# A symmetric product of later batches: one quarter transposed in place of computed, and a bank for each half

## The reference

```python
x = x + attn(layernorm(x))          # linear attention: no softmax
    # theta, phi = x @ W_theta.T, x @ W_phi.T ; g = x @ W_g.T
    # attn = (theta @ phi.T / 16) @ g
x = x + ffn(layernorm(x))
    # rmsnorm, q/k/v (16 heads, 4 key heads of 16), rope,
    # causal softmax attention over the 1024 rows, wo,
    # rmsnorm, gate over 8 experts, top 2, SiLU expert blocks (512 wide)
```

## Time and profile before

| what | value |
|---|---|
| median of three runs | 1089.72 us (1089.57 to 1092.33) |
| the profiled execution | 1089.67 us, of which the span from first to last instruction is 1087.9 |
| PE busy | 1042.4 us (96%) |
| DVE busy | 763.2 us (70%) |
| ACT busy | 581.1 us (53%) |
| POOL busy | 421.9 us (39%) |
| HBM traffic | 55.76 MB read, 41.14 MB written |

### The profile page before, as it was taken

How to read it: one execution, slowest core, us unless ns; L and a number is a source line. 1 busy time by engine, 2 the same in 40 slices (tenths; PEclk the granted TensorE clock), 3 DMA queues, 4 the chain that set the end, 5 groups by cost and what they waited for, 6 DMA issues and landing times.

```text
span 1087.9 us, 19824 instructions
## 1 busy us (share of the span) xinstructions
PE 1042.4 (96%) x6630; PEld 619.5 (57%) x6630; DVE 763.2 (70%) x1811; ACT 581.1 (53%) x1124; POOL 421.9 (39%) x493
## 2 busy tenths in 40 slices
PE   7999999999999999999999999999999999999996
PEld 6765335564435333354333533456667986679996
DVE  4699999768788897788886699243485555555552
ACT  3563566646677887747666566641432244453320
POOL 2020232625643134521434512555637833344332
PEclk9999999999999999999999999999999999999999
DMA  6334113322324656723342511233434432222322
GB/s 192 124 94 122 51 49 106 93 76 77 100 75 140 187 175 193 216 78 99 105 126 85 140 55 37 65 75 74 103 83 98 99 62 38 45 36 40 50 43 27
DMA packets 85732, 101.50 MB, mean 93 GB/s; under 512 B 17632, under 2 KB 73312, under 8 KB 85632
## 3 DMA queue, kind: packets, MB, share of 16 engines
q1 hardware_dynamic: 70752, 80.60, 25.7%
q0 software_dynamic: 14880, 19.64, 9.5%
HBM read 55.76 MB, written 41.14 MB: 89 GB/s over the span
## 4 chain that ended last, share of the span: by engine, by line
PE 70%; DVE 19%; issue 4%; ACT 4%; POOL 1%; DMA 1%; SPq 0%; POOLq 0%; DVEq 0%; ACTq 0%
PE psum L2167 12%; PE psum L2189 9%; PE psum L2119 9%; PE psum L2152 8%; PE psum L2105 7%; DVE psum L1881 7%; PE psum L2085 4%; DVE mx L1883 3%; PE psum L2161 3%; PE psum L2071 3%; PE psum L2126 2%; PE psum L2088 2%; ACT probs_mem L1360 2%; PE psum L2092 2%; PE psum L2038 2%
## 5 line engine op out<-in xcount | busy, mean ns | idle before, releaser
L1360 ACT ACTIVATE probs_mem<-psum 128x512 f32<-128x512 f32 (+1 forms) x464 | 233.6, 585 | 103.3 <-PE psum L2105 98.6
L1881 DVE CUSTOM_DVE_ANT_1 psum<-psum,masking 128x640 f32<-128x640 f32 (+3 forms) x256 | 256.9, 1046 | 31.1 <-PE psum L2088 28.2
L2105 PE MATMUL psum<-stack_mem 98*128 98x512 bf16 (+3 forms) x768 | 170.9, 327 | 6.0 <-ACT probs_mem L1360 2.4
L1259 POOL DMA_INDIRECT out<-yout,labels x68 | 108.9, 1602 | 164.7 <-DVE yout L1961 78.1
L1200 POOL TENSOR_SCALAR_AFFINE_SELECT probs_mem<-probs_mem 128x512 f32<-128x512 f32 x104 | 67.7, 653 | 237.4 <-ACT probs_mem L1360 237.1
L2105 PEld LDWEIGHTS psum<-stack_mem 98*128 98x128 bf16 x768 | 65.0, 97 | 104.5 <-ACT probs_mem L1360 21.5
L1385 ACT ACTIVATE gated<-psum 128x512 f32<-128x512 f32 x68 | 40.6, 597 | 150.9 <-PE psum L2152 68.9
L2119 PE MATMUL psum<-probs_mem,v 128*17 128x512 f32 (+3 forms) x1152 | 116.0, 490 | 0.6 <-ACT heads_out L1367 0.2
L2189 PE MATMUL psum<-w_mem,gated 128*128 x480 | 114.4, 381 | 0.0
L1883 DVE TENSOR_REDUCE mx<-psum 128x4 f32<-128x512 f32 (+2 forms) x96 | 96.6, 1040 | 19.5 <-PE psum L2093 11.8
L2085 PE MATMUL psum<-stack_mem 96*128 96x512 bf16 x256 | 94.8, 383 | 8.6 <-DVE mx L1881 5.1
(11 more groups left out here) (243 smaller groups left out, 1770.1 us busy)
## 6 DMA issues: line engine op xcount, KB each, us to landing
block<-routed SPq DMA_DIRECT2D x68, 129.0 KB
w_mem<-in_w13T SPq DMA_DIRECT2D x16, 512.0 KB, 4.4
qk_parts<-w_mem SPq DMA_DIRECT2D x16, 384.0 KB, 2.6
stack_mem<-qk_parts SPq DMA_DIRECT2D x32, 192.0 KB, 3.0
w_mem<-in_x SPq DMA_DIRECT2D x8, 512.0 KB, 5.3
out<-w_mem SPq DMA_DIRECT2D x8, 512.0 KB, 4.1
x_late<-out SPq DMA_DIRECT2D x8, 512.0 KB, 5.0
stack_mem<-qk_parts SPq DMA_DIRECT2D x32, 128.0 KB, 2.6
```

The source lines that it names most:

```text
L1259: e.indirect_dma_start(out_rows, bass.IndirectOffsetOnAxis(ap=to, axis=0), youts[w % NYOUT], None, bounds_check=NBATCH * SEQ - 1, oob_is_e ...
L1360: e.activation(probs[probs_of(m)][:, hh:hh + n, q0:CH], grid(turn[step][0][:, 0:n * (CH - q0)], n), ACT.Exp, scale=float(HD) ** -0.5).then ...
L1881: e.tensor_tensor_reduce(keys, keys, masked(w), 1.0, -3e38, ALU.add, ALU.max, to).then_inc(sem["max"], 1)
L2105: m = e.matmul(bk[:, i * (CH - q0):(i + 1) * (CH - q0)], s[0:STACK + NMAX, kt // TPR, GRP, kt % TPR * P:(kt % TPR + 1) * P], s[0:STACK + N ...
```

## The change

For batches 1 to 3:

- The first step forms rows 0 to 127 of the Gram matrix as before, 8 products of 128x256.
- The second step forms only the right half of rows 128 to 255: 8 products of 128x128. The left half of these rows is the transpose of the right half of the first rows. Once ACT has copied the first half to SBUF, PE transposes that 128x128 quarter from there into the place in PSUM (one transposition; a new wait on `gram_out`).
- Each half lies in a bank of its own, so a later batch takes two neighbouring banks of the ring, both from before the first product to the copy of the second half.
- ACT copies each half for itself, 128x256, so it has two instructions where it had one, and `gram_out` counts both.
- The plan's costs of the two steps are new: 3.46 and 1.85 on PE in place of 3.46 each, and 0.29 on ACT for each in place of 0.49 once. `needs` is unchanged: the plan doesn't know that the second step waits for ACT's copy of the first half.

Batch 0 is as before; its two parts lay in two banks already.

```diff
--- before.py
+++ after.py
@@ -142,6 +142,8 @@
 
 def gram_steps(b):
 
+
+
     return KD if b else TPB
 
 
@@ -190,8 +192,9 @@
 def work_of(step):
     stage, *at = step
     if stage == "gram":
-        took = ("PE", 0.865 * TPB / gram_steps(at[0]))
-        return (took, ("ACT", 0.49)) if at[1] == gram_steps(at[0]) - 1 else (took,)
+        if at[0]:
+            return ("PE", 1.85 if at[1] else 3.46), ("ACT", 0.29)
+        return (("PE", 0.865), ("ACT", 0.49)) if at[1] == TPB - 1 else (("PE", 0.865),)
     if stage == "split":
         b, c, u, i = at
         return ((("DVE", 0.6) if not b else ("POOL", 1.22), ("ACT", 0.53), ("POOL", 1.13), ("ACT", 0.53), ("DVE", 0.6) if not b else ("POOL", 1.13))[i],)
@@ -574,7 +577,7 @@
 
     def seat(step):
 
-        n = max_banks(*step[3:]) if step[0] == "max" else KD if step[:2] == ("gram", 0) else 1
+        n = max_banks(*step[3:]) if step[0] == "max" else KD if step[0] == "gram" else 1
         at = min(range(RING - n + 1), key=lambda i: max(empty[i:i + n]))
         return at, n
 
@@ -699,7 +702,7 @@
         else:
             done[step] = end + DRAIN[engine] + (FIRST_ROWS if step == ("load_x", 0) else LANDING.get(step[0], 0.0))
 
-        if in_ring and engine in ("DVE", "ACT") and all(e not in ("DVE", "ACT") for e, _ in chain[i + 1:]):
+        if in_ring and not (step[0] == "gram" and not step[2]) and engine in ("DVE", "ACT") and all(e not in ("DVE", "ACT") for e, _ in chain[i + 1:]):
             for s in [("gram", step[1], 0)] if step[0] == "gram" else [step, ("q1_mm", *step[1:])] if step[0] == "q2_mm" else [step]:
                 for k in range(place[s][0], sum(place[s])):
                     empty[k] = end + DRAIN[engine]
@@ -884,7 +887,7 @@
 
 
         emptied = {
-            "pair": lambda s: ("pair_out", 1), "xnT": lambda s: ("xnT_out", nth[s]), "gram": lambda s: ("gram_out", s[1] + 1),
+            "pair": lambda s: ("pair_out", 1), "xnT": lambda s: ("xnT_out", nth[s]), "gram": lambda s: ("gram_out", 2 * s[1] + 1),
             "square": lambda s: ("square_out", nth[s]), "x1": lambda s: ("x1", nth[s]), "hT": lambda s: ("hT_out", nth[s]),
             "v": lambda s: ("v_out", 2 * nth[s]), "k_mm": lambda s: ("rope", 7 * nth[s] - 4), "q1_mm": lambda s: ("rope", 7 * nth[s]),
             "q2_mm": lambda s: ("rope", 7 * nth[s]), "max": lambda s: ("max", nth[s]), "maxT": lambda s: ("neg", 2 * nth[s]),
@@ -1317,9 +1320,13 @@
                         q.wait_ge("v_mm", 2 * (b - 1))
                         q.wait_ge("q2_mm", QR * (b - 1))
                     e.activation(xnT[b % 2][:, :, 2 * c * P:(2 * c + 2) * P], grid(turn[step][0], KD), ACT.Copy).then_inc(sem["xnT_out"], 1)
-                elif stage == "gram" and at[1] == gram_steps(at[0]) - 1:
+                elif stage == "gram":
+                    b, i = at
                     q.wait_ge("gram_mm", nth[step])
-                    e.activation(gram, gram_parts(at[0]), ACT.Copy).then_inc(sem["gram_out"], 1)
+                    if b:
+                        e.activation(gram[:, i], gram_parts(b)[:, i], ACT.Copy).then_inc(sem["gram_out"], 1)
+                    else:
+                        e.activation(gram, gram_parts(b), ACT.Copy).then_inc(sem["gram_out"], 1)
                 elif stage == "square":
                     q.wait_ge("square_mm", nth[step])
                     e.activation((gw, mix)[at[1]], grid(turn[step][0], KD), ACT.Copy).then_inc(sem["square_out"], 1)
@@ -2013,7 +2020,11 @@
                     to = gram_parts(b)
                     q.wait_ge("xn", TPB * (b + 1) if b else i + 1)
                     for j, k in [(j, i) for j in range(TPB)] if b else [(i, k) for k in range(KD)]:
-                        m = e.matmul(to[:, k], xn[b % 2][:, j, k * P:(k + 1) * P], xn[b % 2][:, j], start=(j == 0), stop=(j == TPB - 1))
+                        own = i * P if b else 0
+                        m = e.matmul(to[:, k, own:], xn[b % 2][:, j, k * P:(k + 1) * P], xn[b % 2][:, j, own:], start=(j == 0), stop=(j == TPB - 1))
+                    if b and i:
+                        q.wait_ge("gram_out", 2 * b)
+                        m = e.transpose(to[:, 1, 0:P], gram[:, 0, P:], ident)
                     m.then_inc(sem["gram_mm"], 1)
                 elif stage == "square":
                     b, second = at
@@ -2022,7 +2033,7 @@
                         q.wait_ge("square_out", nth[step] - 1)
                         q.wait_ge("pair_out", 1)
                     else:
-                        q.wait_ge("gram_out", b + 1)
+                        q.wait_ge("gram_out", 2 * b + 1)
                         q.wait_ge("load_wg", 16)
                     for r in range(KD):
                         for k in range(KD):
```

## The result

Ten runs of the changed kernel took 1092.18 to 1095.71 us, median 1092.96. Ten runs of the kernel before, beside them on the same chip, took 1089.52 to 1092.33, median 1090.28. The ratio is 1.0025, with an interval of 1.0015 to 1.0035: about 2.7 us slower, just within the 0.3% called no difference, and on the other side from the forecast of 1085.4. It also lies above the upper end of the range, 1092.0.

A forecast was written before the change was run, and what follows sets the result against it. It took PE as the bound in the expert blocks and at batch 3's product, with batches 1 and 2 beside DVE's work. Saving 4.7 less 0.4 of wait is 4.3: 1089.7 - 4.3 = 1085.4 us, range 1081.5 to 1092.0.

The forecast's parts named there:

- Steps (1) to (4): Gram product, each later batch: first step stays, second saves 1.67 us, transposition adds 0.11, ACT's two copies cost nothing.
- Step (5): PE's transposition waits for ACT's copy of the first half: nothing in batches 1 and 2, 0.4 us in batch 3.
- Step (6): Two neighbouring banks of seven held from first product to second half's copy: taken 0, bounds 0 and 1.5 us.
- rival C: Held banks starve attention's first heads and DVE's idle time grows by 9.5 us: 1094.9 us, slower, chance 0.13.
- Step (7): The plan is made anew: PE's gain goes to later work beside DVE's; shifted waits and seven fewer fillers cost nothing.
- taken as 0: Small PE waits shifted by the new order, 54.4 to 571.2 us: 2 us either way, counted as nothing.
- the whole saving arrives: All three batches' 4.7 us, less 0.4 of wait, reaches the end: chance 0.53, own range 1083 to 1087.5 us.
- rival A: Batches 1 and 2's saving is lost beside DVE's work, leaving batch 3's 1.56 less 0.4: 1088.5 us, chance 0.27.

The follow-up runs named there:

- e18: Changed kernel with ACT's planned half-copy cost 0.38 for 0.29, second Gram step wide again, no transposition: 1090.90 us, 0.9999 of the kernel before.
- e2: Changed kernel's plan and banks, with the second Gram step wide again and no transposition: 1093.75 us, 1.0040 of the kernel before.
- e14: Changed kernel with planned costs 2.0 (PE, second step) and 0.38 (ACT) in place of 1.85 and 0.29: 1087.36 us, 0.9976 of the kernel before.
- e1: Kernel before, same order, second Gram steps narrow in batches 1 to 3, quarter transposed from the previous batch (wrong values): 1090.94 us, ratio 1.0013.
- e4: Whole change put into the kernel before's order, ACT's added copy, both halves in one bank: 1090.84 us, ratio 1.0012.
- e13: Changed kernel with ACT's planned half-copy cost 0.38 in place of 0.29: 1086.57 us, 0.9979 of the kernel before.
- e9: Changed kernel with e8's repeats and a few more ahead of the clock fall at 360 us: 1090.91 us, 1.0025 of the kernel before.
- e12: As e9, but with the second Gram step wide and no transposition: 1095.47 us, 1.0059 of the kernel before.
- e17: Kernel before with the planned cost of a Gram product at 0.83 in place of 0.865: 1090.85 us, ratio 1.0017.
- e8: Changed kernel with some PE instructions repeated in idle time ahead of the clock falls: 1089.07 us, 0.9997 of the kernel before.
- e6: Kernel before with e1's narrow second Gram step in batches 1 and 2 only: 1088.03 us, ratio 1.0007.

## Why the prediction was wrong

**Steps (1) to (4) held.** A narrow step took 1.79 us (taken 1.78) and its transposition 0.11 (0.11); ACT's halves took 0.37 and 0.38 us and nothing waited behind them. **Step (5)** cost 0 in place of 0.4. **Step (6)**, the pair of banks, has no run of its own. e18 holds the pairs with the old work in nearly the old order and is at 0.9999 of the kernel before, so no cost of them can be measured there. DVE's idle time from 54.4 to 163.2 us is 108.8 - 101.7 = 7.1 us against 6.3, so rival C's mechanism didn't happen, though C's sign came out. The range's upper end counts the 0.4 us of wait twice; by its own terms it is 1091.6.

**Step (7) failed**, in both its parts.

First, "taken as 0" for the new order. e2 has that order with the old work, and is 0.40% slower, 4.4 us; the step said 2 us at most. That the order costs this is shown. What in it costs it is shown in part. It shifted small waits of PE into six of 1.5 to 2.3 us in e2, where the longest before are 1.25 and 1.21 us, and behind two of them stand 3.4 and 6.8 us at half the clock. The forecast had read the clock of the earlier trace rows, 1.00 everywhere, as a constant, and no term or rival had it change.

A fall's price has two readings. Between profiles of one order it is 1.3 to 1.6 us for 3.4 us at half the clock, and less where PE would have waited anyway (2.2 for 6.8 us in e18, nothing at 192 us in the changed kernel). Between runs of one kernel, those with a lower mean are longer by 1.4 to 2.1 us (the kernel before: 1088.83 and 1090.26, 1088.55 and 1090.06, 1088.84 and 1090.91, at 0.997 and above and at 0.995 to 0.996). That second reading isn't the clock's alone, for between 0.998 and 0.997 it turns round: in all five sets the runs at 0.997 are shorter, by 0.2 to 1.0 us. e2's profile has 10 us at half the clock, three falls' worth, so 4 to 5 us by the first reading (an estimate). The falls can be all of what this order costs, but the waits by themselves aren't excluded, and from one order to another the time doesn't follow the falls (e14).

Second, "the whole saving arrives". It rested on PE doing later work in the gap beside DVE. Batch 1's 1.56 us doesn't arrive in any order: from its first Gram step to batch 2's it is 33.29 us before and 33.27 in e1, 32.41 in e2 and 32.59 in the changed kernel. Batch 2's becomes waits and then a fall of the clock in the old order's profiles; in the new orders 1.1 to 1.5 us of it arrive. Of batch 3's, 0.6 us arrive in the old order by the profiles (1.0 by the runs without a fall) and 1.6 in the new ones. So rival A's mechanism holds for batch 1 everywhere and for batch 2 in one order of three, and its forecast of 1.2 us kept is near what e1 and e4 show without a fall, 1.2 to 1.5. The saving isn't a number of the change alone; it depends on the order around it. By the medians alone that wouldn't be shown: 1.6 us (the changed kernel against e2), 2.2 (e13 against e18) and 3.7 (e9 against e12) have intervals that overlap.

**Together:** the order's 4.4 us less the 1.6 that the narrow step gives back in it are the 2.7 measured, within rounding; against the forecast of 4.3 us saved, 4.4 of the miss is the order, 3.1 the part of the 4.7 that didn't arrive, less the 0.4 of wait that didn't come. The profiles split it otherwise. Up to 250 us the changed kernel has 3.0 us from its narrow steps that e2 lacks, and behind 430 us it loses 3.1 in the four waits that no other kernel of its order has. Their cause is open. So is what makes e14, with two falls of 6.8 us each in its profile, as fast as e13.

The weakest reasoning was to price a new plan by the size of the edit. e17 changes no work, only a planned cost by 4%, and is 1.8 us slower. The chance for that should have been far larger than the 0.06 that it had for moving the full saving above 1086.4, and the range wider at its upper end.

## What to carry to other kernels

Products that PE does beside a slower engine may save nothing when they are taken out, and without them PE may idle long enough that the clock falls: look at the granted clock in narrow cuts around the edit, and ask how long PE will be idle there without them. Where a planner sets the order, a change of cost makes a new order with a price of its own, here up to 5 us for the same work: measure a few plans, and the old work in the new order, before the change is judged. Fill idle time of PE only where the trace shows it, and measure again; 16 fillers by the plan came with 5 to 6 us here, and repeats by the trace took back in two of four places what they gave. Before a gain is put down to an edit, follow the same instructions in both profiles from the start: 1.3 us of e8's lead over the changed kernel were there before the edit, and 3.1 came behind it.

## What the runs showed of the hardware

PE's clock fell in the middle of a kernel in which PE is busy 95% of the time, for 3.4 or 6.8 us at once, behind stretches of 3.4 to 3.7 us in which PE had been busy 1.5 to 1.8. It doesn't fall behind each of them: e2 has one of 3.5 us with PE busy 1.24, and the clock stays at 1.00. At half the clock sixteen records of the second product of attention took 3.17 us in the changed kernel, at the full clock 1.70 in e8:

```profile
192.17 3.17 PE L2130 MATMUL psum<-probs_mem,v 128*17 128x512 f32 x16
```

```profile
190.88 1.70 PE L2134 MATMUL psum<-probs_mem,v 128*17 128x512 f32 x16
```

The Trainium skill (TensorE: Matmul & The Clock Gate, Part 1: The HAM clock gate) says that the clock has two levels, that idleness lowers it and work raises it again. By that rule the trace agrees: 1.00 and 0.50 are the levels here, and every fall ahead of the tail stands behind waits of PE, though not every such wait has a fall behind it. The page of the profile doesn't show them: it has a 9 in every slice of PE's clock.

One program doesn't fall at the same places in every run: e6 had means from 0.991 to 0.998 in twelve runs, and times from 1087.69 to 1094.49. A median over a few runs of such a kernel says little; the spread of the clock beside it says more.
